# Four of six stages of a fused decoder in one block, with a rearranged opening of the first attention

## What is computed

```
x = x + _L0_attn_ref(_layernorm(x), ...)                 # attention, 16 heads of 16, LoRA on q, k, v, o
x = x + _L0_xattn_ref(ctx_2048, ctx_2048, _layernorm(x)) # long convolution
x = x + _L0_ffn_ref(_layernorm(x), ...)                  # LoRA experts, best 2 of 8
x = x + _L1_attn_ref(_layernorm(x), ...)                 # wide attention, 16 heads of 128, causal
x = x + _L1_xattn_ref(_layernorm(x), ctx_2048, ...)      # linear attention
x = x + _L1_ffn_ref(_layernorm(x), ...)                  # mix of 32 experts
```

## Time and profile before

| | us |
|---|---|
| median of 3 runs | 1017.61 (1017.22 to 1017.93) |
| the profiled execution | 1014.11 |
| its span, first to last instruction | 1012.3 |
| PE busy in it | 953.7 (94%) |
| mean granted clock of TensorE | 0.977 |

### The profile page before, as it was taken

The page is one execution under the profiler, slowest core; times in us unless marked ns, Lnnn a source line. Parts: engine busy times, 40 slices in busy tenths (PEclk is TensorE's granted clock), DMA queues, the critical chain, the costliest instruction groups (busy, mean ns, idle before and its releaser), DMA issues.

```text
span 1012.3 us, 19821 instructions
## 1 busy us (share of the span) xinstructions
PE 953.7 (94%) x7441; PEld 821.8 (81%) x7441; DVE 643.7 (64%) x1376; ACT 483.2 (48%) x1613; POOL 262.2 (26%) x239
## 2 busy tenths in 40 slices
PE   7899998999787999999999999999999998999877
PEld 5677775999666888988889888888888886777757
DVE  5678887698876575544644445444454467777853
ACT  3778885432233555444444434444444454554431
POOL 3455774560541222211111102111021123110000
PEclk9999998999898999999999999999999999999979
DMA  8000000000301222100000000000000023000002
GB/s 303 5 2 3 2 2 1 23 1 1 104 1 45 63 63 63 53 1 1 2 1 1 1 2 1 1 1 1 1 1 1 22 91 146 1 3 1 1 1 84
DMA packets 12076, 27.89 MB, mean 28 GB/s; under 512 B 1936, under 2 KB 7088, under 8 KB 11344
## 3 DMA queue, kind: packets, MB, share of 16 engines
q1 hardware_dynamic: 11264, 26.42, 7.5%
q10 hardware_dynamic: 720, 0.20, 0.1%
HBM read 24.52 MB, written 2.10 MB: 26 GB/s over the span
## 4 chain that ended last, share of the span: by engine, by line
PE 64%; ACT 2%; DVE 2%; issue 1%; POOL 0%; DVEq 0%; ACTq 0%
PE bank L42 14%; PE bank L43 13%; PE bank L44 13%; PE bank L1388 6%; PE bank L1337 5%; PE bank L1378 3%; PE bank L1882 2%; PE bank L1895 2%; PE bank L2344 1%; PE bank L1872 1%; PE bank L143 1%; PE bank L1861 1%; PE bank L2404 1%; PE bank L2379 1%; DVE li_rden L2088 1%
## 5 line engine op out<-in xcount | busy, mean ns | idle before, releaser
L1312 POOL TENSOR_TENSOR wa_prob<-wa_prob,wa_rsum 128x512 f32<-128x512 f32 x64 | 75.6, 1181 | 431.7 <-DVE wa_rsum L1563 431.7
L42 PE MATMUL bank<-norm_xT_hi,wide_hi 128*128 128x512 f32 x256 | 107.0, 418 | 3.3 <-ACTq L1525 3.3
L1468 ACT ACTIVATE wa_prob<-wa_prob,wa_negmax 128x128 f32<-128x128 f32 x256 | 100.0, 392 | 16.7 <-DVE wa_negmax L1552 16.4
L1597 DVE TENSOR_TENSOR le_w_or_z_lo<-bank,le_w_or_z_hi 128x512 fp32r<-128x512 f32 x64 | 44.2, 691 | 94.8 <-ACT le_w_or_z_hi L1509 94.1
L44 PE MATMUL bank<-norm_xT_hi,wide_lo 128*128 128x512 f32 x256 | 102.0, 399 | 0.0
L43 PE MATMUL bank<-norm_xT_lo,wide_hi 128*128 128x512 f32 x256 | 102.0, 398 | 0.0
L1489 ACT COPY wa_v<-bank 128x512 f32<-128x512 f32 x64 | 37.5, 585 | 127.5 <-PE bank L44 127.4
L521 ACT ACTIVATE v_or_conv<-bank,la_negmax 128x128 f32<-128x128 f32 x256 | 90.4, 390 | 3.2 <-PE bank L359 2.0
L1558 DVE COPY wa_k<-bank 128x512 f32<-128x512 f32 x64 | 44.2, 691 | 64.4 <-PE bank L44 64.3
L1476 ACT COPY wa_q<-bank 128x512 f32<-128x512 f32 x64 | 37.5, 586 | 99.3 <-PE bank L44 99.3
L281 POOL TENSOR_TENSOR v_or_conv<-v_or_conv,la_rsum 128x512 f32<-128x512 f32 x64 | 66.5, 1040 | 61.2 <-DVE la_rsum L589 61.1
(11 more groups left out here) (314 smaller groups left out, 2497.1 us busy)
## 6 DMA issues: line engine op xcount, KB each, us to landing
h_or_w<-in_wide_w SPq DMA_DIRECT2D x11, 512.0 KB, 4.3
li_em_w<-in_em_w SPq DMA_DIRECT2D x1, 4096.0 KB, 14.2
x<-in_x SPq DMA_DIRECT2D x4, 512.0 KB, 5.1
lc_kt<-in_ctx_rev SPq DMA_DIRECT2D x1, 2048.0 KB, 10.4
lc_toep<-in_toeplitz SPq DMA_DIRECT2D x1, 2048.0 KB, 14.7
wa_v<-in_wide_w SPq DMA_DIRECT2D x4, 512.0 KB, 6.7
out_x<-x SPq DMA_DIRECT2D x8, 256.0 KB, 2.6
li_kt<-in_ctx_rev SPq DMA_DIRECT2D x1, 1536.0 KB, 7.5
```

What stands on the lines that cost most here:

```text
L42: nc.tensor.matmul(out, a[0], b[0], start=start, stop=False, skip_group_check=True)
L1312: nc.gpsimd.tensor_tensor(prob[:, s], prob[:, s], rsum[:, s, :].unsqueeze(2).to_broadcast([P, G, P]), ALU.mult).then_inc(prob_ok, 1)
L1468: last = nc.scalar.activation(prob[:, s, j, :], prob[:, s, j, :], ACT.Exp, bias=negmax[:, s, j:j + 1], scale=SCALE, accum_out=sums[:, s, j ...
L1597: nc.vector.tensor_tensor(z[1][:, t % 2, :], b_z[:, :], z[0][:, t % 2, :].bitcast(F32), ALU.subtract).then_inc(z_lo, 1)
```

## The change

**One block.** Convolution, experts, wide attention, linear attention and mix become one block (`run_stages`); only the boundary between first attention and convolution keeps its block end and clearing. `long_conv` and `lora_experts` return their five programs and a record of events (`ConvDone`, `ExpertsDone`). Each place that writes early over something a former stage still reads waits for its own event: SP's loads, ACT's first copies, PE's first products on two of the banks, DVE's additions. The last sums of the convolution go to `b_c[2:4]` in place of `b_c[0:2]`, and three raw weight pieces get room of their own (`le_raw`) over the convolution's products. POOL waits for `norm.s_xn` before it adds `outs` to x.

**Opening of the first attention.** x is loaded ahead of the LoRA factors. These lie in 4 x 32 partitions (`lora_a`, `lora_b`, zero-padded on the host), and PE takes the four weights in turn in its four row groups. `ORDER` is q, k, v, o: DVE folds q and k first, v and o after the split of k. PE's scores of the first four units and the bias products go ahead of `values`; ACT makes two units' exponentials ahead of `keep_v`. POOL adds the first group's bias in units 2 to 5.

**Loop of the first attention.** `STATS_AT, RSTD_AT, APPLY_AT` go from 3, 5, 7 to 2, 4, 6. In the last group `o_rest` goes ahead of `row_max`.

```diff
-        STATS_AT, RSTD_AT, APPLY_AT, BIAS_AT = 3, 5, 7, 10
+        STATS_AT, RSTD_AT, APPLY_AT, BIAS_AT = 2, 4, 6, 10
-        ORDER = (2, 0, 1, 3)
+        ORDER = (0, 1, 2, 3)
...
+            load_x(sp, 0)
             sp.dma_start(lora_b[:], io["l0_b"]).then_inc(lora_loaded, 16)
             sp.dma_start(lora_a[:], io["l0_a"]).then_inc(lora_loaded, 16)
-            load_x(sp, 0)
...
-            pool.wait_ge(bias_ok, 1)
-            for j in range(G):
-                add_bias(0, j)
...
+                if 2 <= n < 2 + G:
+                    if n == 2:
+                        pool.wait_ge(bias_ok, 1)
+                    add_bias(0, n - 2)
...
+            for c in range(DC):
+                for n in range(4):
+                    rows = slice(32 * n, 32 * n + 32)
+                    last = nc.tensor.matmul(b_s[n][:, c * D:(c + 1) * D], lora_b[rows, c * P:(c + 1) * P],
+                                            lora_a[rows, :], start=True, stop=True)
+            last.then_inc(w_ps, 1)
...
+            scores(0)
+            scores(2)
             pe.wait_ge(w_f32, 4)
...
-                if m == 1:
+                if m == 0:
                     for c in range(DC):
                         norm.hi_chunk(act, 0, c, b_p[c], xT[0][0])
...
+            exps(0)
+            exps(1)
             act.wait_ge(v_zero, 1)
             for half in range(2):
                 keep_v(0, half, b_p[half])
-            exps(0)
-            exps(1)
...
+            fold(0)
+            fold(1)
...
+                if n == 2:
+                    fold(2)
+                    fold(3)
...
+                if g >= NG - 1:
+                    o_rest_due(n)
                 if n + 3 < N:
                     row_max(n + 3)
...
-            return b_c[0:2] if i == NG - 1 else b_x
+            return b_c[2:4] if i == NG - 1 else b_x
...
+            sp.wait_ge(*conv_done.products_read)
             for i, (n, b) in enumerate(PIECES):
                 sp.dma_start(raw[i], wide_part(io["wide_w"][n], n, b)).then_inc(wide_in[i], 16)
+            sp.wait_ge(*conv_done.slots_read)
...
+            pool.wait_ge(norm.s_xn, norm.done(NG))
             for j in range(G):
                 pool.wait_ge(out_kept, j + 1)
...
+                    elif j in conv_done.bank_free:
+                        pe.wait_ge(*conv_done.bank_free[j])
...
+            pe.wait_ge(*conv_done.le_lo)
             products(0, first)
...
             apply(1)
+            dve.wait_ge(*conv_done.x_pool)
             norm.vector_stats(dve, 2)
...
+            sp.wait_ge(*experts_done.gates_ok)
             sp.dma_start(causal[:], io["causal"]).then_inc(loaded, 16)
+            sp.wait_ge(*experts_done.h_ps)
```

More of the change, by code:

```diff
@@ L445, in _ @@
                 turn_x(0, c, b_p[c])
+            pe.wait_ge(norm.s_lo, DC * norm.split(0))
+            pe.wait_ge(w_lo, 2)
+            for m in range(DC):
+                q_or_k(0, m, 0, b_p[m], q_ps)
+            for m in range(DC):
+                pe.wait_ge(q_ok, m + 1)
+                q_or_k(0, m, 1, b_p[m], k_ps)
+            scores(0)
+            scores(2)
             pe.wait_ge(w_f32, 4)
@@ L451, in _ @@
             last.then_inc(bias_ps, 1)
-            pe.wait_ge(norm.s_lo, DC * norm.split(0))
-            pe.wait_ge(w_lo, 2)
-            for m in range(DC):
-                q_or_k(0, m, 0, b_p[m], q_ps)
             pe.wait_ge(w_lo, 3)
-            for m in range(DC):
-                pe.wait_ge(q_ok, m + 1)
-                q_or_k(0, m, 1, b_p[m], k_ps)
             for half in range(2):
@@ L769, in _, with tensor_program @@
             pool.wait_ge(x_pool, G)
-        @block.tensor
-        def _(pe):
+        def tensor_program(pe):
+            norm.enter_stage(1, 0, b_n)
             def conv(i):
@@ L823, in _, with scalar_program @@
             sum_slots(NG - 1)
-        @block.scalar
-        def _(act):
+        def scalar_program(act):
+            norm.enter_stage(1, 0, b_n)
             def squares(i):
@@ L859, in _, with vector_program @@
             norm.scalar_hi(act, NG)
-        @block.vector
-        def _(dve):
+        def vector_program(dve):
+            norm.enter_stage(1, 0, b_n)
             def add_sums(i):
@@ L1022, in _, with tensor_program @@
             pool.wait_ge(x_pool, G)
-        @block.tensor
-        def _(pe):
+        def tensor_program(pe):
+            norm.enter_stage(2, 1, b_p)
             def products(it, batches):
@@ L1665, in all_stages @@
         pr.wide_raw = [pr.wide_v[:, 1, 2 * i:2 * i + 2, :] for i in range(2)]
[L1666 to L1669 removed]
+        experts, experts_done = lora_experts(pr, conv_done)
+        wide, wide_done = wide_attention(pr, experts_done)
+    with ExitStack() as ctx:
+        linear, opening, mix = linear_attention(pr, ctx, wide_done)
+        run_stages(pr, conv, experts, wide, linear, opening, mix)
 def linear_attention(pr, ctx, wide_done):
```

152 lines of the change are left out of this document (94 added, 58 removed).

## The result

There were four executions of each kernel. The changed kernel took 1004.87 us (median; 1003.63 to 1007.39), the kernel before 1017.41 (1012.32 to 1017.93). The ratio is 0.9891, with an interval of 0.9854 to 0.9928. The forecast was 1004.8 us within 1000.0 to 1011.0. The profiled execution took 1005.10 us at a mean granted clock of 0.982; its span is 1003.3 us, 9.0 less than that of the kernel before, which ran at 0.977.

What follows compares the result with a forecast made beforehand. PE, busy 94% of the span, bounds the kernel; gains were sought in its idle times and low clock. Work 8.7 us, plus 4.5 for the clock, less 0.4, makes 12.8: 1017.6 - 12.8 = 1004.8 us, range 1000.0 to 1011.0.

Steps and rivals of the forecast that it cites:

- The opening: First attention's start: earlier x, two folds instead of four and v's products in PE's hole gain 2.2 us (0.5 to 2.6).
- the discount for the clock: First attention's start: if PE reaches full clock at the same instant although it begins earlier, half of 1.9 us is lost.
- The clock at 34: First attention, 33.7 to 37.1 us: with PE's 2.6 us hole filled, the low stretch goes, gaining 1.7 us (0 to 1.7).
- The last group: First attention's end: shorter waits for oT_lo gain 1.2 us (0 to 2.1), the low clock after them 2.8 (0 to 3.4).
- Convolution to experts: Boundary after the convolution: PE starts the experts without the block's end, 2.4 us gained (1.1 to 3.4), half the clock's included.
- Experts to wide attention: Boundary gone and POOL held back for DVE: 2.9 us (1.7 to 3.2); low clock from 315.5 us: 2.3 (0 to 2.4).
- A low stretch at a new place: No place named: 0.4 us taken off the forecast gain in case the clock falls somewhere new.
- The rule that the prediction weighed: Low-clock places: the gate's window is free-running, so a shorter hole may still be punished, at the old or a new place.
- rival (a): Whole kernel: the clock is low as often as before, at old or new places; 8.7 us remain, near 1009.7; chance 0.21.
- Rival (b): Merged boundaries and last group: the time goes to the next late item; gain 7.3 us, or 1010.3; chance 0.10.
- (d): Whole kernel: slower, idleness spread so that the clock falls more often, from six more low stretches; near 1020; chance 0.03.
- (e): Whole kernel: time within 0.2% of before, with five more low stretches; chance 0.03.

Runs made afterwards that it cites:

- late exponentials: The changed kernel with ACT's first two sets of exponentials behind its two copies of v, as in the kernel before: 1009.50 us, ratio 0.994.
- Merging alone: The kernel before with its first attention kept and the later blocks merged as in the changed kernel: 1011.67 us, ratio 0.9957.
- the attention alone: The kernel before with the changed first attention (opening and loop) and the rest in four blocks as before: 1010.05 us, ratio 0.9953.

## Why the prediction was right, and where not

**The opening** (2.2 us, bounds 0.5 to 2.6): 3.13, above the upper bound. Two steps were off. The loads gave 1.7 us and not 0.9, of which 0.5 went to a load that comes last, and 2.27 us were won at the first projection, not 1.9. And the discount for the clock was wrong. The first products run 0.43 us apart and the later ones 0.235, and the change between the two came at 20.0 us before and at 17.9 after; it moved with the start of the work, so nothing was lost there. The way from the first projection to the first turn was 14.73 us, and the prediction had 14.9. The late exponentials show that ACT's order is needed for all of it; what the loads and the folds give was not run by itself, but PE works nearly without a pause between its first projection and its first turn (one wait of 0.87 us), so their 2.27 us pass through.

**The clock at 34** (1.7 us): the stretch went, as said. But from the first turn to the copy of unit 48 only 0.5 us came of it. This doesn't price the clock, as the two loops differ. Merging alone does, as it has the attention of the kernel before: there the interval took 112.26 us with 2.8 held back in it, against 111.25 with 1.7. So 1.1 us held back cost 1.0, and the 1.7 some 1.6 (an estimate from this pair). The changed loop then lost about 1 us of the opening's 3.13 again. It shows in the first units (the copy of unit 2 comes 6.14 us after the first turn, before 6.70, of which 1.7 were held back); which wait takes it was not isolated.

**The last group** (1.2 for the waits and 2.8 for the clock): 1.35 in all, and this is the step that failed. The prediction named the row maximum and DVE's copy as next in line and still took 1.2 us for the whole. The copy's waits rose by 2.0 us as oT_lo's fell by 1.9. Undone, the edit gives 0.8 us more. The prediction took the two halves, earlier statistics and oT's rest ahead of the row maximum, as one gain, and they work against each other. With the old order the early statistics brought the waits for oT_lo from 3.0 to 2.0 us and left the copy's at 1.6; the swap then added 2.0 for the copy and took 0.9 off. That the statistics alone are worth some 0.9 us is an estimate: before, 31.48 us with 3.4 held back, less 1.4 us for each 1.7 (28.7 to 30.1 in the changed kernel), is 28.6 to 28.7, and with early statistics and the old order it was 27.8. With the swap in place they give nothing, in the one comparison there is. The low stretch did not go but halved, and in other executions of the same instructions it is absent or five times as long. By the same estimate what was gained here in this pair is clock alone: 1.7 us less held back, 1.35 us less time. A low clock here with no wait ahead of it was one of the marks that the prediction set against itself, and the trace comes near it: ahead of the stretch at 161 us PE's longest wait in this group was 0.8 us.

**Convolution to experts** (2.4 us, bounds 1.1 to 3.4): 2.73 to the first rest of an experts' tile, the place that the prediction named. The hole of "some 2.5 us" behind two tiles is 2.22, and the low clock behind it is there, as it feared.

**Experts to wide attention** (2.9 and 2.3 for the clock): 3.02 and 2.17. POOL's wait is worth 1.33 by the kernel without it, the merged block the rest; the attention alone, with separate blocks, has the old 7.28.

**A low stretch at a new place** (0.4 us): two came. The one at 294 cost 1.24 us, from h's turn to the applications. It stands behind a hole of 1.9 us which the kernel before had too, and no low stretch followed it there. The rule that the prediction weighed, that a low clock depends on how the work happens to lie, fits the seven of ten. The one at 949 has no edit near it: from the load of `em_simT` to the first store the same code took between 171.4 and 173.7 us in the fourteen profiles, with 8.5 or 10.2 held back, and not in the order of these.

**The sum.** The terms of plain work were 2.2 + 1.2 + 2.4 + 2.9 = 8.7 us; measured are 3.13 + 0 + 2.73 + 3.02 = 8.9. An error of 0.9 in the opening and one of 1.2 in the last group nearly cancel, and that is luck. (If the opening's later loss of about 1 us, estimated above, is counted as work, it is 7.8.) For the clock it had 4.5 - 0.4 = 4.1; the profiled pair gives no more than 0.1 (1.2 by the other count), the new stretches having eaten most of the old ones' gain. That is rival (a), which asked for 1009.7. The medians say otherwise. Taken as span times what is missing of its mean clock, the kernel before held back 24.4 us (the median of 36 executions), the changed one 17.0 (of nine), and their times are 1015.6 and 1003.6, 12.0 apart. By this measure the profiled executions held back 23.3 and 18.1: the one before is somewhat better than its kernel's median, the one after somewhat worse. The prediction left the 3.5 us between the profiled time before and the median as they were, and was right to. So of some 12 us about 8 to 9 are work, read from intervals, and the other 3 to 4 fit the 7 us that are held back less. That last part is a reckoning from medians, over different chips, and no experiment shows it by itself.

Rival (b) is refuted at the boundaries, where nothing late took the time over, and confirmed in the last group. (d) and (e) asked for five or six low stretches more than before; there were fewer. Of the marks that the prediction set, wide attention 11 to 13 us earlier was missed in the profile (8.8), by the last group and the stretch at 294, and the convolution some 6 us earlier too (5.0, by the copy of unit 63).

## What to carry to other kernels

When the engine that serves the late item serves others too, putting that item first moves the wait; add up all of the waiting engine's waits before and after, not the one that was aimed at. Price a low clock by what the same instructions took at either level, not by its length: 1.7 us held back cost 1.24 and 1.29 us in the experts and 1.45 to 1.48 in the last group, and 8.5 cost 6.5 there. And count how often a low stretch is there before it is put down to an edit: with the same instructions it came and went. And once a hole of about two us on PE can't be closed by reordering, products that nobody reads, put into it with no wait of their own, are a cheap thing to try: both delayed nothing here, and what they gain is the clock's, in the times shown only together with the order on DVE.

## What was not expected of the hardware

- The opening's eight small LoRA products (16 records) take 2.09 us from four strips of 32 rows of the array, 7.19 from one strip of 16 (timeline, after and before): 0.26 us each in place of 0.90. It lies beside other work and is not in the sum. The row after:

```profile
5.98 2.09 PE L442 MATMUL bank<-la_lora_a,la_lora_b 32*128 32x256 f32 x16 [5.98 <-DMA la_lora_a<-in_l_a]
```

- The granted clock reads 1.00 from 14 to 22 us while the products of 512 columns start 0.43 us apart and then 0.235. The trace's first clock record lies at 20.1 us before and at 18.0 after, just where the spacing changes; ahead of it the column has nothing to read. So it does not show the slow start of the engine; the products' spacing does.
- The clock fell behind idle times of PE of 1.9 and 2.2 us, and in the last group behind six of 0.8 or less; that last place gave anything from no low stretch to one of 17 us, with the same instructions.
